# A two-stage attention and ternary feed-forward kernel: small VectorE operations go to GpSimd, the value-sum turning becomes a transpose, and the squares of the feed-forward stage are folded once more

## The reference

```
x = x + layernorm(attn(layernorm(x)))        # 16 heads of 128, causal softmax
    q = rope(x Wq^T);  kv = x Wkv^T
    kh, vh = cumsum(x Wkvh^T * exp(cumsum(log_sigmoid(x Wg^T))))   # 16 + 16 columns
    k[n,h,:] = rope(kp[n,:] * kh[n,h]);  v[n,h,:] = vp[n,:] * vh[n,h]
    softmax(q k^T / sqrt(128), causal) v, all heads, times Wout^T
x = x + layernorm(ffn(layernorm(x)))
    w' = w + (ternary(w) - w)                # in bf16, one scale for each 64 weights
    gate, up = x Wgu'^T;  h = silu(gate) * up          # 1024 columns each
    h = h * rsqrt(mean(h*h) + eps);  h Wproj'^T
```

## Time and profile before

| what | value |
|---|---|
| median of three runs | 1093.43 us |
| the profiled execution's own time | 1093.13 us |
| its span, first to last instruction | 1091.3 us |
| TensorE busy in the span | 1052.3 us, 96% |
| GpSimd busy | 928.1 us, 85% |
| VectorE busy | 872.8 us, 80% |
| ScalarE busy | 861.5 us, 79% |
| mean granted TensorE clock | 0.996 of full speed |

### The profile page before, as it was taken

How to read it: one execution, slowest core, us unless ns; L and a number is a source line. 1 busy time by engine, 2 the same in 40 slices (tenths; PEclk the granted TensorE clock), 3 DMA queues, 4 the chain that set the end, 5 groups by cost and what they waited for, 6 DMA issues and landing times.

```text
span 1091.3 us, 25312 instructions
## 1 busy us (share of the span) xinstructions
PE 1052.3 (96%) x8010; PEld 1006.2 (92%) x8010; DVE 872.8 (80%) x2870; ACT 861.5 (79%) x2386; POOL 928.1 (85%) x846
## 2 busy tenths in 40 slices
PE   6899999999999999999999999999999899999997
PEld 6798999899989998998999999999999799999997
DVE  6879889989998998899889988987877656666654
ACT  4787888888888888887888788888878666666674
POOL 4698999899989999998999899999899658777685
PEclk9999999999999999999999999999999999999999
DMA  7450211021112110221021112111130000000001
GB/s 264 163 167 29 59 42 59 22 68 60 47 34 59 61 39 31 59 61 46 24 70 58 40 38 71 41 40 59 30 117 21 2 1 21 20 21 20 21 20 39
DMA packets 35124, 58.57 MB, mean 54 GB/s; under 512 B 3136, under 2 KB 16000, under 8 KB 34688
## 3 DMA queue, kind: packets, MB, share of 16 engines
q1 hardware_dynamic: 34992, 56.96, 16.6%
HBM read 50.92 MB, written 9.18 MB: 55 GB/s over the span
## 4 chain that ended last, share of the span: by engine, by line
POOL 59%; PE 21%; issue 17%; ACT 1%; DVE 1%; POOLq 0%; DMA 0%; ACTq 0%; DVEq 0%
POOL arena L575 15%; POOL arena L607 14%; POOL arena L596 14%; POOL arena L585 13%; PE psum L910 11%; PE psum L940 5%; PE psum L721 1%; PE psum L920 1%; PE psum L969 1%; POOL arena L545 1%; POOL X L566 1%; POOLq L297 0%; PE psum L747 0%; POOL arena L552 0%; PE psum L826 0%
## 5 line engine op out<-in xcount | busy, mean ns | idle before, releaser
L607 POOL TENSOR_TENSOR arena<-arena 128x768 f32<-128x768 f32 x128 | 196.5, 1535 | 18.8 <-DVE arena L1419 17.5
L575 POOL TENSOR_TENSOR arena<-arena,tables 128x512 f32<-128x512 f32 x128 | 165.7, 1295 | 39.4 <-ACT arena L1090 39.1
L585 POOL TENSOR_TENSOR arena<-arena 128x512 f32<-128x512 f32 x128 | 188.7, 1474 | 10.0
L1432 DVE SCALAR_TENSOR_TENSOR pt_split<-psum,vh_col,pt_split 128x256 fp32r<-128x256 f32 (+1 forms) x512 | 176.9, 407 | 0.0
L596 POOL TENSOR_TENSOR arena<-arena 128x512 f32<-128x512 f32 x128 | 165.2, 1290 | 2.6 <-DMA arena<-kh_rows 1.7
L826 PE MATMUL psum<-arena 128*128 128x256 f32 x512 | 154.6, 384 | 8.4 <-POOL arena L585 8.4
L1101 ACT ACTIVATE arena<-arena 128x256 f32<-128x256 f32 x256 | 128.6, 502 | 32.3 <-DVE arena L1409 25.5
L721 PE MATMUL psum<-wo_hi,o_hi 128*128 128x256 f32 x512 | 152.7, 298 | 0.0
L721 PE MATMUL psum<-xt_hi,wq_hi 128*128 128x256 f32 x512 | 146.0, 285 | 0.0
L721 PE MATMUL psum<-xt_lo,wq_hi 128*128 128x256 f32 x512 | 144.9, 283 | 0.0
L721 PE MATMUL psum<-xt_hi,wq_lo 128*128 128x256 f32 x512 | 144.9, 283 | 0.0
(11 more groups left out here) (170 smaller groups left out, 3508.1 us busy)
## 6 DMA issues: line engine op xcount, KB each, us to landing
arena<-kh_rows SPq DMA_DIRECT2D x127, 256.0 KB, 3.3
out<-spare SPq DMA_DIRECT2D x15, 256.0 KB, 2.1
arena<-w_rows SPq DMA_DIRECT2D x6, 512.0 KB, 4.7
X<-L_attn_Wout SPq DMA_DIRECT2D x1, 2048.0 KB, 14.5
X<-L_attn_x SPq DMA_DIRECT2D x1, 2048.0 KB, 13.0
arena<-L_attn_Wq SPq DMA_DIRECT2D x1, 1536.0 KB, 10.1
X<-L_attn_x SPq DMA_DIRECT2D x1, 1536.0 KB, 10.2
w_rows<-L_ffn_w_gate_up SPq DMA_DIRECT2D x3, 512.0 KB, 9.3
```

The lines of the kernel that those rows point to most:

```text
L575: nc.gpsimd.tensor_tensor(swap, swap, spread, ALU.mult).then_inc(q_sined, 1)
L585: nc.gpsimd.tensor_tensor(q_rot[p % 2], q_cos[p % 2], q_swap[p % 2], ALU.add).then_inc(q_roped, 1)
L607: nc.gpsimd.tensor_tensor(tb, tb, r.unsqueeze(3).to_broadcast([P, HP, 3, P]), ALU.mult).then_inc(p_ready, 1)
L1432: last = nc.vector.scalar_tensor_tensor(pt_lo[p % 2][:, o], b[:, i], vh[:, t, h:h + 1], pt_hi[p % 2][:, o].bitcast(F32), ALU.mult, ALU.sub ...
```

## The change

It moves `bias_x` and `bias_y` to GpSimd, as a multiplication by -1 beside the variance sum and a product behind the power. It moves `weights_scale` to GpSimd, one step earlier, and the weight `change` a step later. `weigh_kv` writes back into PSUM, `sum_kv` reads it there in step 5, and the value projection, which overwrites that bank, waits for the scan. `turn_vh` becomes a transpose. In the feed-forward stage GpSimd adds the last two tiles of squares (`fold_squares`), TensorE sums one tile and does so behind up chunk 2, GpSimd takes `invert_z` last, ScalarE normalises z behind chunk 1, and VectorE takes the floor of z last. The first batch's table shifts some stages by a step.

The tables and GpSimd's functions:

```diff
-             decay_a=3, decay_b=4, coef=5, weigh=5, sum=6, store=6, values=5, values_hi=6, values_lo=6, vh=7)
...
+             decay_a=3, decay_b=4, coef=5, weigh=5, sum=5, store=6, values=5, values_hi=6, values_lo=6, vh=7)
...
-WSTEP = dict(cast=1, sum=2, scale=3, above=8, below=10, decide=15, sign=16, change=16, finish=17, turn=23, copy=23,
+WSTEP = dict(cast=1, sum=2, scale=2, above=8, below=10, decide=15, sign=16, change=17, finish=17, turn=23, copy=23,
...
+                nc.gpsimd.tensor_tensor(ln1_minus, ln1_agg[:, :, 0], minus_one, ALU.mult).then_inc(ln1_neg, PAIRS)
                 pool.wait_ge(ln1_eps, c0 + PAIRS)
                 nc.gpsimd.tensor_tensor(ln1_rstd, ln1_rstd, minus_half[:, 0:NT], ALU.pow).then_inc(ln1_inv, PAIRS)
+                pool.wait_ge(ln1_inv, c0 + PAIRS)
+                pool.wait_ge(ln1_neg, c0 + PAIRS)
+                nc.gpsimd.tensor_tensor(ln1_bias, ln1_minus, ln1_rstd, ALU.mult).then_inc(ln1_biased, PAIRS)
...
+
+            def weights_scale(g0, s):
+
+                c0 = chunk_at(g0, s, "scale")
+                if c0 is not None:
+                    pool.wait_ge(wt_summed, chunks_done(c0))
+                    nc.gpsimd.tensor_scalar(w_scale, w_sums, 1.0 / GROUP, 1e-8, ALU.mult, ALU.max).then_inc(wt_scaled, ROUND)
+                    nc.gpsimd.tensor_scalar(w_half, w_sums, 0.5 / GROUP, 0.5e-8, ALU.mult, ALU.max)\
+                        .then_inc(wt_scaled, ROUND)
+                    nc.gpsimd.tensor_scalar(w_below, w_sums, -0.5 / GROUP, -0.5e-8, ALU.mult, ALU.min)\
...
+            def fold_squares(u, i):
+
+                pool.wait_ge(h_summed, u + 1)
+                nc.gpsimd.tensor_tensor(squares[i][:, 0, :], squares[i][:, 0, :], squares[i][:, 1, :], ALU.add)\
+                    .then_inc(h_folded, 1)
...
                     split_hidden(*at, 1)
+                at = unit_at(u0, s, FLAG["sum"])
+                if at and not last_unit(at[0]):
+                    fold_squares(*at)
+                at = unit_at(u0, s, FLAG["z"])
+                if at and last_unit(at[0]):
+                    invert_z(*at)
+                at = unit_at(u0, s, FLAG["up"])
+                if at:
+                    split_hidden(*at, 2)
                 at = unit_at(u0, s, FLAG["out"])
                 if at and not last_unit(at[0]):
                     add_x(*at)
+                at = unit_at(u0, s, FLAG["up"])
+                if at:
+                    split_hidden(*at, 3)
                 at = unit_at(u0, s, FLAG["z"])
-                if at:
+                if at and not last_unit(at[0]):
                     invert_z(*at)
-                at = unit_at(u0, s, FLAG["up"])
-                if at:
-                    split_hidden(*at, 2)
-                    split_hidden(*at, 3)
 
```

TensorE, ScalarE and VectorE:

```diff
-                pe.wait_ge(kvw_done, c0 + PAIRS)
+                pe.wait_ge(cum_done, c0 + PAIRS)
...
-                    last = nc.tensor.matmul(F_BANK[:, t * 2 * H:(t + 1) * 2 * H], kv_cum[par][0:2 * H, t * P:(t + 1) * P],
-                                            ident[0:2 * H, 0:2 * H], start=True, stop=True)
+                    last = nc.tensor.transpose(F_BANK[:, t * 2 * H:(t + 1) * 2 * H], kv_cum[par][0:2 * H, t * P:(t + 1) * P],
+                                               ident[0:2 * H, 0:2 * H])
                 last.then_inc(vh_turned, PAIRS)
...
                     u, i = at
                     down(u, i)
-                    if not last_unit(u):
-                        pe.wait_ge(h_summed, u + 1)
-                        sum_tiles(u, i, range(FC))
                 at = unit_at(u0, s, FLAG["up"])
                 if at:
                     up(*at, 2)
+                at = unit_at(u0, s, FLAG["sum"])
+                if at and not last_unit(at[0]):
+                    u, i = at
+                    pe.wait_ge(h_folded, u + 1)
+                    sum_tiles(u, i, (0,))
...
 
             def step(u0, s):
-                at = unit_at(u0, s, FLAG["out"])
-                if at:
-                    norm_z(*at)
                 at = unit_at(u0, s, FLAG["up"])
                 if at:
                     activate(*at, 0)
                     high_hidden(*at, 0)
                     activate(*at, 1)
                     high_hidden(*at, 1)
+                at = unit_at(u0, s, FLAG["out"])
+                if at:
+                    norm_z(*at)
...
-                nc.vector.tensor_tensor(kvw[rows, :], F_BANK[rows, N:2 * N], coef[rows, :], ALU.mult)\
+                nc.vector.tensor_tensor(F_BANK[rows, N:2 * N], F_BANK[rows, N:2 * N], coef[rows, :], ALU.mult)\
                     .then_inc(kvw_done, PAIRS)
...
-                nc.vector.tensor_tensor_scan(kv_cum[par][rows, :], ones[rows, :].to_broadcast([2 * H, N]), kvw[rows, :], 0.0,
-                                             ALU.mult, ALU.add)\
+                nc.vector.tensor_tensor_scan(kv_cum[par][rows, :], ones[rows, :].to_broadcast([2 * H, N]), F_BANK[rows, N:2 * N],
+                                             0.0, ALU.mult, ALU.add)\
                     .then_inc(cum_done, PAIRS)
...
                     nc.vector.bn_stats(z_stat[:, t, :], Z_BANK[i][:, t * E:(t + 1) * E]).then_inc(z_stats, 1)
-                if not last_unit(u):
-                    sum_floor(u, i)
                 dve.wait_ge(z_stats, u * NT + NT)
                 for t in range(NT):
...
                     multiply(*at, 3)
+                at = unit_at(u0, s, FLAG["z"])
+                if at and not last_unit(at[0]):
+                    sum_floor(*at)
 
```

More of the change, by code:

```diff
@@ L54 @@
 FRONT = dict(turn=0, split=0, split_lo=1, keys=1, gates=2, gates_one=2, key_swap=2, key_cos=3, key_sin=3, key_rope=4,
-             decay_a=3, decay_b=4, coef=5, weigh=5, sum=6, store=6, values=5, values_hi=6, values_lo=6, vh=7)
[L56 to L62, removed]
+             decay_a=3, decay_b=4, coef=5, weigh=5, sum=5, store=6, values=5, values_hi=6, values_lo=6, vh=7)
+AHEAD = dict(stats_a=3, stats_b=4, invert=5, norm_a=6, norm_b=7)
+FIRST = dict(stats_a=0, stats_b=0, invert=0, norm_a=1, norm_b=1, turn=2, split=2, split_lo=3, keys=3, gates=4,
+             gates_one=4, key_swap=4, key_cos=5, key_sin=5, key_rope=6, decay_a=5, decay_b=6, coef=6, weigh=6, sum=6,
+             store=6, values=6, values_hi=7, values_lo=7, vh_late=7)
+TAIL = dict(copy=5, stats=7, invert=7, norm_a=11, norm_b=12, add=14)
+TAIL_LAST = dict(copy=5, stats=6, invert=6, norm_a=7, norm_b=7, add=7)
 FLAG = dict(stats=0, norm=1, turn=1, up=2, sum=3, down=3, z=3, out=4)
@@ L154, in sandwich_kernel @@
         coef = carve(N)
-        kvw = carve(N)
+        carve(N)
         kv_cum = [carve(N) for _ in range(2)]
@@ L288, in sandwich_kernel @@
             sem(k) for k in ("z_stats", "z_aggr", "z_eps", "z_neg", "z_inv", "z_biased", "z_norm", "res_done"))
-        tile_done = sem("tile_done")
+        tile_done, h_folded = sem("tile_done"), sem("h_folded")
         stored = [sem(f"stored{i}") for i in range(2)]
@@ L701, in batch @@
                         residual(c0)
+                    weights_scale(g0, s)
                     place_down(g0, s)
@@ L987, in batch @@
                         turn_vh(0, 0)
+                    c0 = front_at(g0, s, "vh_late")
+                    if c0 is not None:
+                        turn_vh(c0, 1 - par)
                     c0 = front_at(g0, s, "keys")
@@ L1646, in batch @@
                         coefs(c0)
-                    c0 = front_at(g0, s, "sum")
-                    if c0 is not None:
-                        sum_kv(c0, 1 - par)
                     c0 = tail_at(g0, s, "stats")
@@ L1677, in batch @@
                         weigh_kv(c0)
-                    c0 = front_at(g0, s, "sum_late")
+                    c0 = front_at(g0, s, "sum")
                     if c0 is not None:
@@ L1698, in batch @@
                         copy_vh(0, 0)
+                    c0 = front_at(g0, s, "vh_late")
+                    if c0 is not None:
+                        copy_vh(c0, 1 - par)
                     for i in later_turns(g0, s):
```

39 lines of the change are left out of this document (10 added, 29 removed).

## The result

The changed kernel takes 1143.66 us, the median of four runs (1141.69 to 1145.8), against 1094.7 for the kernel before in the same runs: a ratio of 1.0442 [1.0423, 1.0461], 49 us slower. The forecast was 1115 us, 21.8 above its starting point of 1093.13. The profiled execution has a span of 1142.8 us, 51.5 more than before.

A forecast was written before the change was run, and what follows sets the result against it. It took GpSimd to set the attention stage's pace, and TensorE plus an equally long ScalarE/VectorE ring the feed-forward stage's. 1093.13 - 8.8 (attention) + 30.6 (feed-forward) = 1114.9, predicted 1115 us; 8-in-10 range 1100 to 1135 us.

The forecast's parts named there:

- the new ring: Feed-forward step: chain through `invert_x2`, low part, fold, sum, turn and up chunk 3 takes 14.89 us against 13.08.
- The feed-forward term: Feed-forward stage: 13 steps each 2.35 us longer because TensorE waits for the fold, +30.6 us (23.5 to 37.7).
- the middle, 2.35 us: Step lengthening between 1.81 us without and 2.90 us with a collision of VectorE's second sum of squares.
- The last two folds zero: Last two folds, without `invert_x2`: the 0.40 us saved and a shorter wait set at zero.
- The attention sum: Attention stage: scale operations, biases and scan together -8.8 us, between -13.8 and +7.3.
- Scale operations: Attention, step 3 of odd batches: moving them off VectorE saves 2.09 us in each of six chunks, -12.5 us.
- Scan: Attention: operand in PSUM ends the delay of GpSimd's operation beside it, 0.26 us in 14 batches, -3.6 us.
- Turning: Attention: 64 matmuls become 32, half of 10.0 us off TensorE; taken as zero, with -5.0 kept for the range.
- Biases: Attention: two further GpSimd operations cost 0.25 us for 14 batches ahead and 15 outputs, +7.3 us.
- The fold is in time: Rival, feed-forward: fold ready before up chunk 2 ends, no added wait, 1078 to 1084 us; chance 0.10.
- VectorE's relief buys nothing: Rival, attention: the 2.09 us go to another wait and GpSimd keeps its additions, 1131 us; chance 0.14.
- The wait is mostly absorbed: Rival, feed-forward: ring has more slack, steps grow by 1 us or less, 1084 to 1097 us; chance 0.06.

The follow-up runs named there:

- e13: Changed kernel with 28 useless up matmuls ahead of TensorE's wait for the fold: 1138.18 us, ratio 1.0402 to the kernel before.
- e10: e9 with the weights' three scale operations back on VectorE in step 3: 1084.22 us, 11.8 above e9.
- e11: e9 with the weighted heads written to an SBUF tile again and the scan reading them there: 1082.35 us, 9.9 above e9.
- e12: e9 with the value-sum turning as a matmul with the identity again instead of a transpose: 1079.21 us, 6.8 above e9.
- e8: e7 with both biases of the layernorms back on VectorE: 1069.53 us, 11.9 below e7.
- e7: e3 with the weights' `change` back at step 16: 1081.39 us, 6.6 below e3.
- e3: Changed kernel with the `fold_squares` call moved ahead of `invert_x2` on GpSimd: 1087.94 us, ratio 0.994 to the kernel before.
- e9: e8 with the first batch's table as before the change: 1072.42 us, ratio 0.9799 to the kernel before.
- e6: Changed kernel with VectorE's second sum of squares behind the last product and 10 useless matmuls in TensorE's wait: 1133.35 us.
- e14: Changed kernel with VectorE's second sum of squares behind the last product and 20 useless matmuls in TensorE's wait: 1126.23 us.

## Why the prediction was wrong

The direction was right, and so was the new ring; two sizes were not, and one effect was missing from the sum. The time lies outside the range. Of the 29.7 us between the 21.8 of the forecast and the 51.5 of the profile, 18.9 are in the feed-forward steps and 10.8 in the attention stage and at the ends. By the prediction's own steps:

**The feed-forward term, +30.6 forecast, +49.5 measured.** This is the step that failed, in two places. First "both start within 0.1 us by the walk, so I take the middle, 2.35 us": they do start within 0.1 us, but there was no half. The second `add_squares` collides in every step (1.78 to 1.80 us in the profile after), so the upper end applied, 14.89 + 1.09 = 15.98. The links themselves held: 1.23, 1.28 and 1.23 us to the fold, 0.77 for it (forecast 1.22, 1.28, 1.25, 0.74). Only the sum took 0.61 in place of 0.40, which makes 16.2, and 16.23 is what e13 shows. That is 3.15 us a step more than 13.08, 41 us in 13 steps. Second, the sum had no term for TensorE's clock. The rows before show no pause there, and so no fall; the forecast itself put a pause of up to 3.7 us into each step and priced TensorE behind it at full speed. In the profile after, 220.6 - 13 x 16.23 = 9.6 us are left. Some 3.0 of them are the fourth step's own, which was 1.0 longer than the others before the change as well (14.08 us). The other 6.6, about 0.5 us a step, go with the falls of the clock; e13, which has one fall in place of ten, gave 5.7 back between the down projections. 41, 2.0 and 6.6 make up the 49.5 to within 0.1.

**"The last two folds zero"** and the free `invert_z` and z held within 1 us: the last two distances are 12.34 and 8.11 us, 0.5 and 0.45 less than before, which is what the halved sum gives.

**The attention sum, -8.8 forecast, about zero measured.** *Scale operations*, -12.5: held to the tenth in the profiles (2.08 us in six steps; 11.8 us in e10), and the additions on GpSimd were absorbed, as the walk took them (L617 to L617 over them 7.07 us, 7.06 before). *Scan*, -3.6: right in kind, too small; about 7 us in batches 1 to 13 of e11. *Turning*, 0: too small as well, 4.5 us there in e12. But this was in a kernel that had the other costs removed, so it need not be its worth inside the changed kernel. *Biases*, +7.3: mis-sized. I priced the additions by an inversion that nothing disturbs, 0.25 us. For the layernorm ahead it is 0.32; for the output's the mean is 2.02 us against 1.01, since the new product is held up in 11 of 15 batches, as by L1495 in the row above, so some 20 us in all on GpSimd's list, against the 7.3 of the forecast. 11.9 us came back in e8; that GpSimd's idle time hid the rest is likely, but not shown. *The weights' `change`*: it is in the diff, and I gave it no price. Together with `finish` in one step it costs 6.6 us (e7).

**The rivals.** "The fold is in time" was refuted for the kernel as written and realised by e3. There its price was wrong: I kept a lower end of no gain, "since the ring of 13.08 us in ScalarE and VectorE stays". The step fell with TensorE's work to 12.62, so the equal length of the two was not two bounds, but ScalarE and VectorE following TensorE, which was busy all the time. "VectorE's relief buys nothing" is refuted by e10. The Trainium skill (Perfetto Trace Analysis, section Optimizing Scalar/DVE Operations) says that moving work between these two engines might not help: it helped for the scale operations (2.08 us a time) and hurt for the biases (11.9 us in all). "The wait is mostly absorbed" is refuted by 37.7 us of waiting.

**What stays open.** The pieces of the attention stage don't add up: undone one by one from e9 they are worth 11.8 + 9.9 + 6.8 us, and the feed-forward part of e3 some 5 us more, 33 in all, while e9 is only 21 below the kernel before. Some 5 of the 33 lie ahead of batch 1, where the profiles differ by up to 5.5 us for a reason that no run shows; which of the others share a wait wasn't tried. Nor was it tried why the clock falls beside some pauses of 1 to 2.4 us and not beside others.

## What to carry to other kernels

When an edit makes the bounding engine wait for a chain on other engines, follow the chain back to what its first member waits for, and place the new work ahead of that: three lines moved turned +49 us into about -7. Price a small operation at its new place, not by its size: on GpSimd, beside a long VectorE operation on two SBUF operands, it can last as long as that one. And look at each changed number of a table as an edit of its own; one that was not priced here ate half of the best gain, and the pieces that cost, sorted out one by one, left a kernel of 1069.53 us, 2.3% below the one before.

## What was not expected of the hardware

TensorE's granted clock falls to half around pauses that stand in an otherwise busy stage: ten stretches of 3.4 or 6.8 us beside waits of 1.4 to 5.5 us in the changed kernel (and none beside three of 2.1 to 2.2 us), seven in e6 beside waits of 1.4 to 1.9 us, and none in eight steps of e14 and of e13, whose waits were 0.54 and 0.27 us. A GpSimd product of two columns took 1.28 us in place of 0.20 beside a VectorE operation of 1.22 us on two SBUF operands.
